# Moving two splits in VectorE's order in a transformer block with mixture of experts

## The chip, the cores and the metric

The kernel runs on one NeuronCore of a Trainium2 chip. The metric is the device time of one execution in microseconds; lower is better. All data is float32.

## The reference

Sixteen sequences of 512 tokens with 256 features pass one transformer block: attention with 16 heads of 64, then a feed-forward part with one shared expert and two of eight routed experts per token. Both parts stand behind a layernorm and are added to their input. Cut to what matters:

```python
def block(x):                                   # x: [16, 512, 256]
    n = layernorm(x)
    q, k, v = heads(n @ Wq.T), heads(n @ Wk.T), heads(n @ Wv.T)
    sim = 50 * tanh(q @ k.T * 64 ** -0.5 / 50)
    attn = softmax(where(causal, sim, -max))
    x = x + merge(attn @ v) @ Wo.T
    t = layernorm(x)
    shared = gelu(t @ sw1 + sb1) @ sw2 + sb2
    probs = softmax(t @ gate_w + gate_b)        # 8 experts, the best 2 are used
    routed = sum(probs[e] * (gelu(t @ w1[e] + b1[e]) @ w2[e] + b2[e]) for e in top2(probs))
    return x + routed + shared
```

## The kernel before

**Stages.** The kernel has two stages. In the first, some 2040 us, it goes through the sequences i = 0 to 15. Attention of a sequence is cut into eight pairs of heads, p = 0 to 7, and the feed-forward front of the sequence before (second layernorm, gate, choice of experts, shared expert) is woven between the pairs. In the second stage it runs the routed experts over gathered tiles of 128 tokens. The change touches the first stage only.

**High and low parts.** To keep float32 accuracy with a faster matmul type, every operand is split: the high part is a cast (`tensor_copy` to F32R), the low part is the original minus the high part. A product is made of high by high, high by low and low by high. Thus most results that leave TensorE's accumulators need a cast (ScalarE or VectorE) and a subtraction (VectorE) before TensorE can use them.

**The ring.** Scores, query and key projections, v, turned tokens, gate, hidden and shared output go through two accumulator slots in one fixed order (`ring_plan`, `AT`). TensorE may fill a slot when its content of two units ago has been emptied (`slot_for`), by ScalarE for scores, v and hidden, otherwise by VectorE. The shared output (`out`) of pair 7 takes the slot in which the queries and keys of the next sequence's pair 0 stood.

**Order.** Each engine runs its own fixed list; semaphores join them. VectorE's list for a pair p is in lines 980 to 1033:

- `weigh_values(i, c)` (L789) multiplies the attention output of chunk c by the inverse denominators; for even c it first takes the reciprocal (L796), the longest instruction of VectorE. A chunk holds half the features of four heads; there are eight per sequence. The chunk weighed in pair p >= 3 is p - 3. Chunks 5, 6 and 7 come in pairs 0 and 1 of the next sequence.
- `split_values(i, c)` (L803) casts the weighed chunk to `oT` high (L808) and subtracts for `oT` low (L810). There is one `oT`, so it waits on `projected` for TensorE's projection of the chunk before (`project_out`, L1268). TensorE projects chunk 6 in pair 2 and chunk 7 in pair 3 behind the scores.
- `empty_qk(i, p + 1)` (L776) makes the low parts of keys (L780) and queries (L785) for the next pair, once ScalarE has cast the high parts (L598, L602). The scores of that pair wait for it (`k_lo`, `dve_emptied`).
- in pair 1 the layernorm of sequence i + 1 (lines 1007 to 1012: statistics L727, Newton steps L748 to L754, application L760); its result is needed by `turn1(i + 1)` in pair 6.
- in pair 3 `add_attention(i - 1)` and the second layernorm; in pair 4 and 5 turned tokens and gate; in pair 6 `choose(i - 1)` (L857) and `split_hidden(i - 1)` (L839), which splits the shared expert's values after gelu for `shared_out` (L1303, high parts from L1305 on); in pair 7 the placing of tokens.

GpSimd masks probabilities and sums them over keys (L508, L520 to L526) for `denominators` (L1238), and sends rows to DRAM (L488, L497). ScalarE does tanh, exp, gelu and high parts. Queries and keys of pair p + 1 are projected in pair p.

Of the kernel before, what the change touches and what calls it, by code (L numbers as in the profile page):

```python
# [118 lines left out]
def block_program(nc, x, wqT, wkT, wvT, woT, gate_w, gate_b_rows, w1s, w1, w2s, w2,  # L119
# [4 lines left out]
    with ExitStack() as ctx:  # L124
# [593 lines left out]
        def _(dve):  # L718
            def split_lo(k):
                name, _ = parts[k]  # L720
                dve.wait_ge(hi_split, k + 1)
                nc.vector.tensor_tensor(split[name][1][:, :], raw[name][:, :],
                                        split[name][0][:, :].bitcast(F32), ALU.subtract).then_inc(lo_split, 1)

            def layernorm_stats(which, src):
                for t in range(NT):
                    last = nc.vector.bn_stats(ln[which]["stats"][:, t, :], src[:, t, :])  # L727
                last.then_inc(ln_steps[which], 1)

            def layernorm_guess(which, i):  # L730
                b, steps, done = ln[which], i * LN_STEPS, ln_steps[which]
                dve.wait_ge(done, steps + 1)
                for t in range(NT):
                    last = nc.vector.bn_aggr(b["mean_var"][:, t, :], b["stats"][:, t, :])
                last.then_inc(done, 1)
                dve.wait_ge(done, steps + 2)
                variance = b["mean_var"][:, :, 1:2]
                nc.vector.tensor_scalar(b["var_eps"][:, :, :], variance, EPS, None, ALU.add)
                nc.vector.tensor_scalar(b["minus_half"][:, :, :], variance, EPS, -0.5, ALU.add,
                                        ALU.mult).then_inc(done, 1)  # L740
                dve.wait_ge(done, steps + 3)
                nc.vector.tensor_scalar(b["rstd"][:, :, :].bitcast(I32), b["var_eps"][:, :, :].bitcast(I32), -0.5,
                                        RSQRT_GUESS, ALU.mult, ALU.add).then_inc(done, 1)
# [32 lines left out]
            def empty_qk(i, p):  # L776
                slot, done = ring[AT["qk", i, p, 0] % 2], 3 * (i * PAIRS + p)
                dve.wait_ge(qk_hi, done + 1)
                for h, r in enumerate(head_rows):
                    last = nc.vector.tensor_tensor(kT[head_rows[1 - h], h, :], slot[r, 1, :],  # L780
                                                   kT[r, h, :].bitcast(F32), ALU.subtract)
                last.then_inc(k_lo, 1)
                dve.wait_ge(qk_hi, done + 2)
                for h, r in enumerate(head_rows):
                    last = nc.vector.tensor_tensor(q_lo[r, h, :], slot[r, 0, :], qT[r, h, :].bitcast(F32),  # L785
                                                   ALU.subtract)
                last.then_inc(dve_emptied, 1)

            def weigh_values(i, c):  # L789

                g, quad = i * PAIRS + c, (i * PAIRS + c) // 2
                if c % 2 == 0:
                    if g >= 1:
                        dve.wait_ge(o_steps, 3 * g)
                    dve.wait_ge(den_done, quad + 1)
                    nc.vector.reciprocal(norm[:, :], bank_d[:, :]).then_inc(inverted, 1)  # L796
                    dve.wait_ge(inverted, quad + 1)
                dve.wait_ge(valued, g + 1)
                if g >= 1:
                    dve.wait_ge(o_steps, 3 * g)  # L800
                nc.vector.tensor_tensor(weighed[:, :], bank_o[:, :], norm[:, :], ALU.mult).then_inc(o_steps, 1)

            def split_values(i, c):  # L803
                g = i * PAIRS + c
                dve.wait_ge(o_steps, 3 * g + 1)
                if g >= 1:
                    dve.wait_ge(projected, g)
                nc.vector.tensor_copy(oT[0][:, :], weighed[:, :]).then_inc(o_steps, 1)  # L808
                dve.wait_ge(o_steps, 3 * g + 2)
                nc.vector.tensor_tensor(oT[1][:, :], weighed[:, :], oT[0][:, :].bitcast(F32),  # L810
                                        ALU.subtract).then_inc(o_steps, 1)
# [16 lines left out]
            def normalise_rows(i):  # L828
                if i >= 1:
                    dve.wait_ge(second_sent, i * NT * 16)  # L830
                layernorm_apply(2, i, row[:, :, TOKEN:TOKEN + D], stream, x2n_ready)
# [7 lines left out]
            def split_hidden(i):  # L839
                dve.wait_ge(act_emptied, EMPTIED[AT["hidden", i, 0, 0]][0])  # L840
                nc.vector.tensor_copy(hT[0][:, :, :], gelu[:, :, :]).then_inc(h_steps, 1)
                dve.wait_ge(h_steps, 2 * i + 1)
                nc.vector.tensor_tensor(hT[1][:, :, :], gelu[:, :, :], hT[0][:, :, :].bitcast(F32),
                                        ALU.subtract).then_inc(h_steps, 1)
# [3 lines left out]
            def empty_logits(i):  # L848
                n = AT["logits", i, 0, 0]
                gates = ring[n % 2][:, 0, 0:NT * E].rearrange("p (t e) -> p t e", t=NT)  # L850
                dve.wait_ge(ring_full, n + 1)
                nc.vector.tensor_reduce(norm1[:, :, :], gates, AX.X, ALU.max).then_inc(gate_steps, 1)
                dve.wait_ge(gate_steps, i * GATE_STEPS + 1)
                nc.vector.tensor_tensor(logit[:, :, :], gates, norm1[:, :, :].to_broadcast([P, NT, E]),
                                        ALU.subtract).then_inc(dve_emptied, 1)
# [124 lines left out]
            for i in range(NSEQ):  # L980
                for p in range(PAIRS):

                    chunk = (i, p - 3) if p >= 3 else (i - 1, p + 5)
                    if p == 2 or chunk[0] < 0:
                        chunk = None
                    if i >= 1 and p == 6:
                        empty_logits(i - 1)
                    if i == 0 and p == 3:
                        dve.wait_ge(idle_padded, 16 * 3)
                    if chunk is not None:  # L990
                        weigh_values(*chunk)
                        if chunk[1] % 2 == 0:
                            split_values(*chunk)
                    if p + 1 < PAIRS:
                        empty_qk(i, p + 1)
                    elif i + 1 < NSEQ:
                        empty_qk(i + 1, 0)
                    if chunk is not None and chunk[1] % 2 == 1:
                        split_values(*chunk)
                    if i == 0 and p <= 1:  # L1000
                        split_lo(3 + p)
                        if p == 1:
                            split_lo(5)
                    if p == 1 and i >= 1:
                        weigh_values(i - 1, PAIRS - 1)
                        split_values(i - 1, PAIRS - 1)
                    if p == 1 and i + 1 < NSEQ:
                        dve.wait_ge(xnext_loaded, 16 * (i + 2))
                        layernorm_stats(1, x_next)
                        layernorm_guess(1, i + 1)  # L1010
                        layernorm_newton(1, i + 1)
                        layernorm_apply(1, i + 1, x_next, x_next, xn_ready)
                    if p == 6 and i + 1 < NSEQ:
                        empty_turned1(i + 1)
                    if i == NSEQ - 1 and p in (4, 5, 6, 7):
                        prepare_bias(p - 4)
                    if i >= 1:
                        if p == 3:
                            add_attention(i - 1)
                            layernorm_guess(2, i - 1)  # L1020
                            layernorm_newton(2, i - 1)
                            normalise_rows(i - 1)
                        if p == 4:
                            empty_turned2(i - 1)
                        if p == 5:
                            empty_gate(i - 1)
                        if p == 6:
                            choose(i - 1)
                            split_hidden(i - 1)
                        if p == 7:  # L1030
                            empty_pos(i - 1)
                            add_shared(i - 1)
                            place_tokens(i - 1)
# [468 lines left out]
```

## Time and profile before

| | us |
|---|---|
| median of 3 runs | 2403.27 (2401.8 to 2406.9) |
| profiled execution | 2412.61 |
| its span, first to last instruction | 2410.9 |
| mean granted TensorE clock | 0.919 of 2.4 GHz |
| TensorE matmul busy | 1987.1 (82%) |
| VectorE busy | 1490.8 (62%) |
| ScalarE busy | 1425.9 (59%) |
| GpSimd busy | 1014.2 (42%) |

The rows come from one profiled execution. A timeline row gives start and duration in us, engine, line and operation, what is written and read, and how many instructions are merged (x); in square brackets stands the idle time of the engine just before, with what ended it. PE is TensorE's matmul, PEld its weight load, DVE VectorE, ACT ScalarE, POOL GpSimd. The granted clock is a share of 2.4 GHz; 0.50 is the level of 1.2 GHz.

### The profile page before, as it was taken

What the parts mean: (1) busy time and instruction counts of PE and PEld (TensorE: products, weight loads), DVE (VectorE), ACT (ScalarE), POOL (GpSimd) and SP (SyncE); (2) the same over time, 40 slices, a digit from 0 to 9 for tenths busy, and PEclk for the clock granted to TensorE, in tenths of its full rate; (3) what the DMA queues carried; (4) which work ended last, traced back from release to release, by engine and by line L of the source; (5) the groups of instructions that cost most, each with busy time, mean ns of one, the idle gap of its engine ahead of it and who ended that gap; (6) DMA issues with size and microseconds to landing.
All of it is one profiled execution on the core that took longest, in us unless ns stands there. A gap on an engine that the chain in (4) does not pass through costs nothing.

```text
span 2410.9 us, 39929 instructions
## 1 busy us (share of the span) xinstructions
PE 1987.1 (82%) x14653; PEld 1577.3 (65%) x14653; DVE 1490.8 (62%) x2803; ACT 1425.9 (59%) x2170; POOL 1014.2 (42%) x1195
## 2 busy tenths in 40 slices
PE   6788888887878788888888788898888885599898
PEld 5566666565656566666666666666665663499898
DVE  4657575756666666666665757575757577566565
ACT  6667475656566665666666657475766562244444
POOL 3434434343434434343434444444343443344344
PEclk9999899999999999999999999899999998699999
DMA  3000000000000000010100000000000002566464
GB/s 114 10 1 18 27 18 27 18 27 10 28 18 19 27 14 31 10 36 10 36 10 27 18 27 18 27 18 27 18 27 10 27 10 84 164 193 186 147 188 138
DMA packets 73665, 112.51 MB, mean 47 GB/s; under 512 B 9715, under 2 KB 52218, under 8 KB 73476
## 3 DMA queue, kind: packets, MB, share of 16 engines
q1 hardware_dynamic: 58468, 67.86, 9.8%
q0 software_dynamic: 15008, 42.10, 4.7%
q8 instruction: 123, 2.02, 0.4%
q14 instruction: 66, 0.54, 0.1%
HBM read 63.10 MB, written 48.65 MB: 46 GB/s over the span
## 4 chain that ended last, share of the span: by engine, by line
PE 52%; DVE 31%; ACT 11%; issue 4%; DMA 1%; another core or an unknown queue 0%; DVEq 0%; POOL 0%; SPq 0%; POOLq 0%; ACTq 0%
PE bank_o L1233 6%; PE ring L1212 6%; DVE q_lo L785 5%; PE ring L1191 5%; PE ring L1217 5%; DVE kT L780 4%; ACT prob L591 4%; PE ring L1139 3%; ACT prob L585 3%; PE ring L1140 3%; PE ring L1145 3%; PE ring L1198 2%; DVE norm L796 2%; ACT kT L598 2%; DVE stats L727 2%
## 5 line engine op out<-in xcount | busy, mean ns | idle before, releaser
L585 ACT ACTIVATE prob<-ring 128x1024 f32<-128x1024 f32 (+1 forms) x384 | 331.8, 880 | 538.2 <-PE ring L1217 533.2
L508 POOL TENSOR_SCALAR_AFFINE_SELECT prob<-prob 128x256 f32<-128x256 f32 x512 | 233.6, 472 | 884.8 <-ACT prob L591 883.9
L1212 PE MATMUL ring<-qT,kT 128*128 128x256 f32 (+3 forms) x1024 | 258.2, 357 | 185.0 <-DVE q_lo L785 133.9
L1212 PEld LDWEIGHTS ring<-qT,kT 128*128 128x128 f32 x1024 | 183.8, 206 | 270.9 <-DVE q_lo L785 133.8
L591 ACT ACTIVATE prob<-prob 128x1024 f32<-128x1024 f32 (+1 forms) x384 | 344.0, 913 | 5.3
L520 POOL TENSOR_TENSOR key_sum<-prob 128x768 f32<-128x768 f32 x128 | 235.2, 1838 | 223.2 <-PE bank_d L1247 211.4
L1233 PE MATMUL bank_o<-prob,v 128*32 128x512 f32 (+3 forms) x4096 | 304.8, 438 | 20.8 <-DVE oTh L808 8.3
L780 DVE TENSOR_TENSOR kT<-ring,kT 64x512 fp32r<-64x512 f32 x256 | 176.4, 689 | 227.4 <-ACT kT L598 224.2
L808 DVE CAST oTh<-weighed 128x512 fp32r<-128x512 f32 x128 | 65.3, 510 | 284.1 <-PE acc L1264 280.8
L1217 PE MATMUL ring<-q_lo,kT 128*128 128x256 f32 (+3 forms) x1024 | 239.1, 336 | 0.0
L1233 PEld LDWEIGHTS bank_o<-prob,v 128*32 128x32 f32 x4096 | 117.1, 110 | 181.0 <-issue 157.6
L796 DVE RECIPROCAL norm<-bank_d 128x512 f32<-128x512 f32 x64 | 214.6, 3353 | 6.2 <-remote 5.2
L1217 PEld LDWEIGHTS ring<-q_lo,kT 128*128 128x128 f32 x1024 | 183.3, 203 | 13.2
L785 DVE TENSOR_TENSOR q_lo<-ring,qT 64x512 fp32r<-64x512 f32 x256 | 176.3, 689 | 8.3 <-ACT qT L602 2.6
L523 POOL TENSOR_TENSOR key_sum<-key_sum,prob 128x512 f32<-128x512 f32 x128 | 169.5, 1324 | 10.0
L598 ACT CAST kT<-ring 64x512 fp32r<-64x512 f32 x256 | 148.1, 579 | 32.5 <-PE ring L1145 31.0
L602 ACT CAST qT<-ring 64x512 fp32r<-64x512 f32 x256 | 148.8, 581 | 24.9 <-PE ring L1145 21.6
L608 ACT CAST qT<-qT 64x512 fp32r<-64x512 f32 x256 | 158.1, 618 | 5.4
L1256 PE MATMUL ring<-w_2h,x2Tl 128*128 128x256 f32 x128 | 55.2, 432 | 121.3 <-DVE q_lo L785 119.2
L1256 PE MATMUL acc<-w_oh,oTh 128*128 128x256 f32 x512 | 132.3, 293 | 0.6 <-DVE oTh L808 0.6
L1258 PE MATMUL acc<-w_ol,oTh 128*128 128x256 f32 x512 | 125.7, 280 | 0.0
L1256 PEld LDWEIGHTS ring<-w_2h,x2Tl 128*128 128x128 f32 x128 | 41.1, 321 | 123.0 <-DVE q_lo L785 120.8
(224 smaller groups left out, 4835.5 us busy)
## 6 DMA issues: line engine op xcount, KB each, us to landing
xin<-first SPq DMA_DIRECT2D x71, 257.0 KB
xin<-second SPq DMA_DIRECT2D x71, 129.0 KB
xin<-base SPq DMA_DIRECT2D x71, 128.0 KB
x_next<-in_x SPq DMA_DIRECT2D x16, 512.0 KB, 4.6
x_res<-in_x SPq DMA_DIRECT2D x16, 512.0 KB, 5.1
raw_e<-in_w SPq DMA_DIRECT2D x4, 1024.0 KB, 6.6
first<-pad SPq DMA_DIRECT2D x9, 257.0 KB, 8.7
second<-pad SPq DMA_DIRECT2D x9, 129.0 KB, 7.7
```

Source lines behind the costliest of these rows:

```text
L508: last = nc.gpsimd.affine_select(out=diag, in_=diag, compare_op=ALU.is_ge, fill=0.0, base=0, pattern=[[0, 2], [1, P]], channel_multiplier=-1)
L520: nc.gpsimd.tensor_tensor(sums[:, :, :], t0[:, :, P:N], t13[:, :, 0:N - P], ALU.add).then_inc(sum_steps, 1)
L585: nc.scalar.activation(probs[p % PROBS][u][:, :, :], slot[:, :, 0:UNIT_COLS[u]], ACT.Tanh, scale=SCALE / SOFTCLAMP).then_inc(act_emptied, 1)
L591: nc.scalar.activation(cols, cols, ACT.Exp, scale=SOFTCLAMP).then_inc(exp_done, 1)
L598: last = nc.scalar.copy(kT[r, h, :], slot[r, 1, :])
L780: last = nc.vector.tensor_tensor(kT[head_rows[1 - h], h, :], slot[r, 1, :], kT[r, h, :].bitcast(F32), ALU.subtract)
L785: last = nc.vector.tensor_tensor(q_lo[r, h, :], slot[r, 0, :], qT[r, h, :].bitcast(F32), ALU.subtract)
L796: nc.vector.reciprocal(norm[:, :], bank_d[:, :]).then_inc(inverted, 1)
L1212: pe.matmul(slot[:, h, to], kT[:, h, keys], qT[:, h, q], start=k == 0, stop=False)
L1217: last = pe.matmul(slot[:, h, to], kT[:, h, keys], q_lo[:, h, q], start=False, stop=k == len(tiles) - 1)
L1233: last = pe.matmul(bank_o[h * QD:(h + 1) * QD, j * P:N], v[:, j, f:f + QD], probs[(2 * quad + h // 2) % PROBS][u][:, h % 2, at:at + N - j ...
L1256: pe.matmul(dst[:, t // 2, t % 2, :], a[0][:, here], w[0], start=start and t % 2 == 0 and k == 0, stop=False)
```

## The change

Two calls in VectorE's list move; no instruction and no wait is added or removed. `split_values(i - 1, 7)` moves from pair 1, where it stood between the weighing of chunk 7 and the layernorm of sequence i + 1, to pair 2, behind `empty_qk(i, 3)`. `split_hidden(i - 1)` moves from behind `choose(i - 1)` in pair 6 to ahead of `empty_qk(i, 7)` in the same pair.

```diff
@@ -991,6 +991,8 @@
                         weigh_values(*chunk)
                         if chunk[1] % 2 == 0:
                             split_values(*chunk)
+                    if p == 6 and i >= 1:
+                        split_hidden(i - 1)
                     if p + 1 < PAIRS:
                         empty_qk(i, p + 1)
                     elif i + 1 < NSEQ:
@@ -1003,6 +1005,7 @@
                             split_lo(5)
                     if p == 1 and i >= 1:
                         weigh_values(i - 1, PAIRS - 1)
+                    if p == 2 and i >= 1:
                         split_values(i - 1, PAIRS - 1)
                     if p == 1 and i + 1 < NSEQ:
                         dve.wait_ge(xnext_loaded, 16 * (i + 2))
@@ -1026,7 +1029,6 @@
                             empty_gate(i - 1)
                         if p == 6:
                             choose(i - 1)
-                            split_hidden(i - 1)
                         if p == 7:
                             empty_pos(i - 1)
                             add_shared(i - 1)
```

## Rows read from the trace of the kernel before

**Rows 1.** Page, part 1: busy time, share of the span, instructions of each engine.

```profile
PE 1987.1 (82%) x14653; PEld 1577.3 (65%) x14653; DVE 1490.8 (62%) x2803; ACT 1425.9 (59%) x2170; POOL 1014.2 (42%) x1195
```

**Rows 2.** TensorE's waits: who for whom, total us, times, longest us.

```profile
PE ring L1212 <- DVE q_lo L785: 133.9, 17, 8.8
PE ring L1256 <- DVE q_lo L785: 119.2, 14, 8.6
```

**Rows 3.** Stretches: start:end, length, engines' busy us, clock, DMA share, GB/s.

```profile
809.68:936.01 126.33, 104.00 (x756) 79.05 (x757) 79.32 (x146) 78.89 (x108) 53.13 (x64) 0.92 0.06 22
...
1820.04:1937.93 117.89, 104.06 (x756) 79.08 (x757) 71.18 (x122) 78.96 (x108) 49.84 (x62) 0.94 0.05 19
```

**Rows 4.** Timeline of VectorE, sequence 6, pair 1 to pair 3.

```profile
780.17 0.69 DVE L801 TENSOR_TENSOR weighed<-bank_o,norm 128x512 f32<-128x512 f32 x1 [1.87 <-remote]
797.23 0.43 DVE L808 CAST oTh<-weighed 128x512 fp32r<-128x512 f32 x1 [16.36 <-PE acc L1264]
...
798.30 1.40 DVE L727 BATCH_NORM_STATS2 stats<-x_next 128x6 f32<-128x256 f32 x4
...
801.02 1.80 DVE L754 SCALAR_TENSOR_TENSOR rstd<-newton,rstd 128x4 f32<-128x4 f32 x1
...
806.82 1.39 DVE L780 TENSOR_TENSOR kT<-ring,kT 64x512 fp32r<-64x512 f32 x2
```

**Rows 5.** Timeline of the other engines in that stretch.

```profile
788.90 0.98 POOL L497 DMA_INDIRECT first<-row,slot_ids  x1 [0.30 <-issue]
...
791.80 1.16 ACT L598 CAST kT<-ring 64x512 fp32r<-64x512 f32 x2
...
800.04 0.86 PE L1247 MATMUL bank_d<-key_sum,ones 128*32 128x384 f32 x8
```

**Rows 6.** Timeline of TensorE, first scores of pairs 3 and 4, sequences 6 and 15.

```profile
809.68 0.79 PE L1212 MATMUL ring<-qT,kT 128*128 128x256 f32 x2 [8.79 <-DVE q_lo L785]
...
821.05 0.47 PE L1212 MATMUL ring<-qT,kT 128*128 128x256 f32 x2 [0.34 <-ACT qT L608]
...
1937.93 0.51 PE L1212 MATMUL ring<-qT,kT 128*128 128x256 f32 x2 [0.38 <-DVE q_lo L785]
...
1947.59 0.48 PE L1212 MATMUL ring<-qT,kT 128*128 128x256 f32 x2 [0.34 <-ACT qT L608]
```

**Rows 7.** Stretches around both stalls; the granted clock is third from the end.

```profile
809.70:813.50 3.80, 3.80 (x13) 3.41 (x14) 3.77 (x2) 2.08 (x3) 0.41 (x1) 0.50 0.00 0
...
871.20:872.20 1.00, 0.00 (x0) 0.00 (x0) 0.97 (x2) 0.00 (x0) 0.92 (x2) 0.73 0.00 0
...
876.70:881.50 4.80, 4.77 (x22) 4.77 (x23) 0.36 (x2) 0.00 (x0) 0.00 (x0) 0.50 0.00 0
```

**Rows 8.** Timeline of VectorE, sequence 6, pairs 6 and 7.

```profile
856.23 1.39 DVE L780 TENSOR_TENSOR kT<-ring,kT 64x512 fp32r<-64x512 f32 x2 [5.90 <-ACT kT L598]
...
866.43 0.69 DVE L841 CAST x2Tl<-gelu 128x1024 fp32r<-128x1024 f32 x1
...
868.38 3.35 DVE L796 RECIPROCAL norm<-bank_d 128x512 f32<-128x512 f32 x1
...
872.49 0.62 DVE L808 CAST oTh<-weighed 128x512 fp32r<-128x512 f32 x1
```

**Rows 9.** Timeline of ScalarE and TensorE in those pairs.

```profile
846.68 1.27 ACT L618 ACTIVATE gelu<-ring,b1s 128x512 f32<-128x512 f32 x2 [2.02 <-PE ring L1145]
...
876.73 0.58 PE L1256 MATMUL ring<-w_2h,x2Tl 128*128 128x256 f32 x1 [8.58 <-DVE q_lo L785]
```

**Rows 10.** Timeline of VectorE: splits beside GpSimd's work, sequences 7 and 15.

```profile
899.86 0.95 DVE L808 CAST oTh<-weighed 128x512 fp32r<-128x512 f32 x1
...
1995.88 2.38 DVE L810 TENSOR_TENSOR oTl<-weighed,oTh 128x512 fp32r<-128x512 f32 x1
```

**Rows 11.** Timeline of TensorE, end of sequence 15.

```profile
2025.91 3.75 PE L1233 MATMUL bank_o<-prob,v 128*32 128x512 f32 x32 [5.84 <-DVE weighed L801]
```

**Rows 12.** Page, part 6: DMA issues, KB each, median us to landing.

```profile
first<-pad SPq DMA_DIRECT2D x9, 257.0 KB, 8.7
```

## Prediction

> **What bounds the kernel now.** I read the page's busy line first, then TensorE's waits, then the span of one sequence, then the timeline around each long wait. TensorE is busy 82% of the span and VectorE 62% [rows 1], so TensorE carries the time and the question is what keeps it idle. The list of its waits has two entries far ahead of the rest, both on the second low-part instruction of VectorE (L785): 133.9 us ahead of score matmuls, 119.2 us ahead of the shared output product [rows 2]. Each is one stall per sequence of about 8.8 and 8.6 us. A sequence lasts 126.3 us from its pair-3 scores to the next sequence's; the last such stretch lasts 117.9 us [rows 3]. That is 8.4 us less, and its one difference up to that point is that sequence 15 normalises no successor in pair 1. The kernel itself thus shows what the first stall is worth.
>
> First stall (sequence 6 as the pattern). VectorE weighs chunk 7 at 780.17 us, then its split stands idle 16.36 us, because the split may overwrite oT only when TensorE has projected chunk 6, at 797.2. Queued behind that split are the layernorm of the next sequence (from 798.30) and the low parts of pair 3 (from 806.82 until TensorE starts) [rows 4]. TensorE finished the denominators at 800.9 [rows 5] and stands 8.79 us until 809.68 [rows 6]. So a wait that concerns nobody in a hurry (chunk 7 is projected only after the scores of pair 3) holds 8.5 us of layernorm and 2.8 us of urgent low parts.
>
> Second stall. In pair 6 and 7 VectorE runs without a gap from 856.23 to 876.7: low parts of pair 7, split of chunk 3, turned tokens, choice of experts, split of the shared values (866.43 to 868.38), reciprocal, weighing and split of chunk 4, low parts of the next sequence's pair 0 [rows 8]. TensorE waits 8.58 us for the last of these, because the shared product needs the ring slot that they empty [rows 9].
>
> **The change part by part.** Nothing is added or removed: 2803 VectorE instructions before and after, no DMA and no wait is new, and the only queue whose order changes is VectorE's own.
>
> Move 1, chunk 7's split (L808, L810, 1.1 us) goes behind the low parts of pair 3. The layernorm then starts at 780.9 and takes the 8.5 us it takes now, up to 789.4. Some of its tiny instructions are stretched now, the longest to 1.80 us [rows 4], while GpSimd sums keys; at the new place it sums the keys of another pair, so I keep the duration. Next come the low parts, which need ScalarE's high part of the keys: that copy starts at 791.80 and takes 1.16 us [rows 5]. So they run from 793.0 to 795.8 and are done 5.0 us before TensorE is free at 800.8. The split waits for 797.2 as before and ends at 798.4, ahead of the reciprocal (801.0) and of its projection (after three score units, about 803.4). The new wait stands in front of the reciprocal only, which needs the denominators of 800.9 anyway. The layernorm has 3.5 us of idle and 5.0 us of slack behind it: it could last 17.1 us, twice its length, before TensorE notices. If that cover were gone, the move would cost one for one. GpSimd issues its last row write to `first` by 789.9 [rows 5]; the residual addition needs it landed, now at 821.1 and then at about 810.5. That leaves 20 us, and writes to `first` of twice that size land in 8.7 us [rows 12].
>
> The stall itself is 8.79 us. Besides, TensorE comes out of it at a granted clock of 0.50, the 1.2 GHz level, for some 3.9 us [rows 7]. From the scores of pair 3 to those of pair 4 it takes 11.37 us in sequence 6; in sequence 15, with no stall ahead, 9.66 us [rows 6]. That is 1.71 us more, and sequence 15 also shows what is late next: pair 4's scores wait 0.34 us for ScalarE, nothing longer. Sum of move 1: 14 sequences (1 to 14) x (8.79 + 1.71) = 147.0 us, and 0.4 us for sequence 15, where the split alone held the low parts.
>
> Move 2, the shared values' split (1.95 us from its start to the reciprocal) goes ahead of pair 7's low parts. After weighing chunk 3 VectorE idles 5.90 us, from 850.33 until 856.23 [rows 8]. The gelu it reads ended at 847.95 [rows 9], so it fits at 850.3 to 852.3 and is hidden by that gap; without the gap it would cost the same 1.95 us that it saves. The chain behind it starts 1.95 us earlier: the denominators, chunk 4's products and ScalarE's copies were all ready several microseconds before VectorE came to them, so none of them ends last instead.
>
> What eats into it: chunk 4's split then meets GpSimd's key sums. Its cast took 0.62 us [rows 8], beside such sums 0.95 us in pair 0 of the next sequence, and a subtraction behind it up to 2.38 us instead of 0.69 [rows 10]. So the loss is between 0 and 1.7 us per sequence. I take 0.5, near the cast's own excess over its undisturbed 0.43 us. The Trainium skill (SBUF — State Buffer, section Who interferes with whom) has VectorE and GpSimd share one port pair as an exclusive lock that a cast takes, so that the second to issue waits for the whole of the other instruction. By that rule the cast would wait for the end of the sum in flight and the subtraction behind it for the next; if it did so for two whole sums, move 2 would bring nothing, which is the second rival below.
>
> Sum of move 2: 14 x (1.95 - 0.5) = 20.3 us. In sequence 15 no low parts hold the product, but the chain leads on to chunk 5's weighing, for which TensorE waits 5.84 us at 2025.91 [rows 11]: 1.9 us.
>
> **Total:** 147.0 + 0.4 + 20.3 + 1.9 = 169.6 us. The profiled execution took 2412.6 us (span 2410.9), so it would take 2243.0. It stands 9.3 us above the median of the runs; the saving is idle time, so I subtract it from the median: 2403.3 - 169.6 = 2233.7 us.
>
> What stays unknown is the clock after the second stall. It shrinks from 8.6 to about 7.1 us; TensorE now runs on at 0.50 for some 5.1 us behind it, and for 3.9 us behind the first [rows 7]. Every sequence gets shorter by a tenth, so where the clock falls and rises against the work will shift. A difference of 1.2 us at half speed is 0.6 us, 14 x 0.6 = 8 us either way. With 0 to 1.7 for the loss the case spans 147.4 + 1.9 + 14 x (0.25 to 1.95) -/+ 8, so savings of 145 to 185 us: 2218 to 2258.
>
> **The rivals.**
> First rival: the clock no longer falls in the shortened second stall. It fell some 3.5 us into the present one (0.73 on average from 871.2 to 872.2 [rows 7]), so 7 us should still do; but were it to stay up, half of 5.1 us comes back as well, 14 x 2.55 = 36 us: 2198 us. Likewise, if the first stall's place left a short wait, nothing would change here. Chance 0.07.
>
> Second rival: move 2 brings nothing, because contention with the key sums takes the whole 1.95 us or another releaser (ScalarE's copies, denominators) holds the low parts. Then 147.4 + 1.9 = 149.3: 2254 us. For it: GpSimd is busy through that stretch and 2.38 us was seen once [rows 10]. Against it: usual excesses are 0.2 to 0.5 us. Chance 0.12.
>
> Third rival: move 1 doesn't do what it says; the stall is held by something that the waits do not name (the v copy, a ring slot), and only move 2 counts: 2403.3 - 22.2 = 2381 us. Against it stands sequence 15, where exactly this stall is 0.38 us. Chance 0.03.
>
> Fourth rival, slower: the layernorm at its new place runs beside GpSimd's key sums and its four indirect row writes, and they stretch it. Up to 17.1 us nothing shows; from there each further microsecond comes out of TensorE, and at 17.1 + 12.0 = 29.1 us the gain of both moves is gone. At 32 us it would be 14 x 2.9 = 41 us slower: 2444 us. Now its longest stretch is 1.80 us for one tiny instruction [rows 4], so this needs a dozen of them. Chance 0.01.
>
> **How the numbers follow.** The forecast has 0.77, the rivals 0.07, 0.12, 0.03 and 0.01. Likeliest: 2233.7 us. Range: 2210 to 2258; it holds the forecast and the second rival and leaves out the other three. A difference of 0.2%, about 5 us, is what a measurement of this kernel can tell from none. Every case but the fourth is faster by more: faster 0.98, same 0.01 (the fourth short of its end), slower 0.01.
>
> **What would show it.** In the profile after: the wait of score matmuls on L785 (133.9 us) falls below 20 us, and the split's idle time of 16 us before it shrinks to about 1.3 us; the layernorm (L727 on x_next) follows the weighing of chunk 7 directly; a sequence lasts 126.3 - 10.5 - 1.5 = 114.3 us; the wait of the shared product falls from 8.6 to about 7.1 us each; the clock is 1.00 over pair 3. Wrong would be: a new wait of over 1 us ahead of pair 3's or pair 7's scores, a layernorm of over 17 us, or a second stall that stays at 8.6.

## The result, and the profile after

The changed kernel takes 2226.96 us (median of 4 runs, 2224.22 to 2230.45), the kernel before 2403.4 us (2401.8 to 2406.9). The ratio is 0.9265, with a 95% interval of 0.9247 to 0.9283. The saving at the medians is 176.4 us, where 169.6 us were forecast; 2227.0 lies inside the range of 2210 to 2258. The profiled execution took 2224.22 us, with a span of 2222.5 us and a mean granted clock of 0.955 (0.919 before).

Page of the changed kernel, part 1 (to compare with [rows 1]):

```profile
PE 1945.4 (88%) x14653; PEld 1539.9 (69%) x14653; DVE 1501.1 (68%) x2803; ACT 1421.8 (64%) x2170; POOL 1004.9 (45%) x1195
```

The counts are the same, as announced. TensorE is busy 88% of the span instead of 82%, and 41.7 us shorter in total: that part isn't idle time but matmuls that ran at a higher clock. VectorE grew by 10 us. Nearly all of it stands in the splits of the weighed chunks, whose subtractions (L810) take 101.6 instead of 93.7 us and whose casts (L808) take 66.9 instead of 65.3; what they meet at their new time is shown at the end of this section.

TensorE's waits of the changed kernel (who for whom, total us, times, longest us), to compare with [rows 2]. The edit moved TensorE's lines down by two: scores are L1214 now, the shared product L1258.

```profile
PE ring L1258 <- DVE q_lo L785: 98.9, 14, 7.1
PE ring L1214 <- DVE x2Tl L773: 20.4, 15, 7.8
...
PE ring L1214 <- DVE q_lo L785: 10.5, 2, 7.9
```

The scores' wait of 133.9 us is down to 10.5 us, in two waits that both belong to the start of the kernel (22 and 71 us into it). The shared product's wait went from 119.2 to 98.9 us, or from 8.5 to 7.07 us each. The 20.4 us for L773 were there before as well (20.6 us). What is new are single waits of under 3 us in the last sequence.

VectorE's timeline of the changed kernel, sequence 6, pair 1 to pair 3 (start, us, instruction, idle time before it), to compare with [rows 4]:

```profile
712.05 0.69 DVE L801 TENSOR_TENSOR weighed<-bank_o,norm 128x512 f32<-128x512 f32 x1
712.65 1.40 DVE L727 BATCH_NORM_STATS2 stats<-x_next 128x6 f32<-128x256 f32 x4
...
714.58 1.84 DVE L739 TENSOR_SCALAR minus_half<-mean_var 128x4 f32<-128x4 f32 x1
...
719.84 1.38 DVE L760 TENSOR_SCALAR x_next<-x_next,mean_var,rstd 128x256 f32<-128x256 f32 x4
726.70 1.39 DVE L780 TENSOR_TENSOR kT<-ring,kT 64x512 fp32r<-64x512 f32 x2 [5.48 <-ACT kT L598]
728.12 1.39 DVE L785 TENSOR_TENSOR q_lo<-ring,qT 64x512 fp32r<-64x512 f32 x2
730.93 0.43 DVE L808 CAST oTh<-weighed 128x512 fp32r<-128x512 f32 x1 [1.42 <-PE acc L1266]
731.39 0.69 DVE L810 TENSOR_TENSOR oTl<-weighed,oTh 128x512 fp32r<-128x512 f32 x1
734.73 3.36 DVE L796 RECIPROCAL norm<-bank_d 128x512 f32<-128x512 f32 x1 [2.64 <-PE bank_d L1249]
```

The layernorm (L727 to L760) follows the weighing of chunk 7 with no gap and takes 8.6 us. The low parts of pair 3 are done at 729.5, 5.0 us before TensorE is free. The split idles 1.42 us where it idled 16.36 us, and its end at 732.1 leaves 2.6 us to the reciprocal. TensorE's timeline of the same sequence, first scores of pair 3 and of pair 4, and the stretch that they bound (start:end, length, busy us of PE, PEld, DVE, ACT, POOL, granted clock, DMA share, GB/s):

```profile
734.53 0.50 PE L1214 MATMUL ring<-qT,kT 128*128 128x256 f32 x2
...
744.19 0.47 PE L1214 MATMUL ring<-qT,kT 128*128 128x256 f32 x2 [0.34 <-ACT qT L608]
```

```profile
733.50:744.19 10.69, 10.35 (x96) 7.19 (x85) 8.19 (x8) 8.43 (x12) 8.25 (x9) 1.00 0.00 0
```

Pair 3 starts with no wait at a clock of 1.00, and pair 4 follows after 9.66 us: to the hundredth what sequence 15 of the kernel before showed [rows 6], and 1.71 us less than its sequence 6.

VectorE's timeline of the changed kernel, the same sequence, pairs 6 and 7 [rows 8], and the shared product that it releases [rows 9]:

```profile
773.37 0.69 DVE L841 CAST x2Tl<-gelu 128x1024 fp32r<-128x1024 f32 x1
...
779.36 1.39 DVE L780 TENSOR_TENSOR kT<-ring,kT 64x512 fp32r<-64x512 f32 x2 [4.04 <-ACT kT L598]
...
789.56 3.35 DVE L796 RECIPROCAL norm<-bank_d 128x512 f32<-128x512 f32 x1
...
793.67 0.64 DVE L808 CAST oTh<-weighed 128x512 fp32r<-128x512 f32 x1
794.35 1.09 DVE L810 TENSOR_TENSOR oTl<-weighed,oTh 128x512 fp32r<-128x512 f32 x1
```

```profile
798.34 0.58 PE L1258 MATMUL ring<-w_2h,x2Tl 128*128 128x256 f32 x1 [7.05 <-DVE q_lo L785]
```

The split of the shared values sits in the gap, which shrank from 5.90 to 4.04 us. In the chain behind it the subtraction of chunk 4 took 1.09 us instead of 0.69. GpSimd's timeline beside it shows why:

```profile
792.76 1.26 POOL L523 TENSOR_TENSOR key_sum<-key_sum,prob 128x512 f32<-128x512 f32 x1
794.11 0.79 POOL L526 TENSOR_TENSOR key_sum<-key_sum,prob 128x256 f32<-128x256 f32 x1
```

The cast, issued at 793.67, finds a sum in flight that ends at 794.02, and itself ends 0.29 us later, at 794.31. The subtraction finds the next sum, which ends at 794.90, and itself ends at 795.44. Undisturbed the two take 0.43 and 0.69 us, so each ends 0.14 or 0.15 us earlier than if its work had begun only when the sum in flight was over.

### The profile page after: what moved, and what is told of

It is laid out like the page before. It is cut to its first block, busy times and chain, and to the rows that moved or that the text cites. A ratio compares the mean times of both kernels' runs of the same rounds, so it can differ in the third digit from the quotient of the medians.

```text
span 2222.5 us, 39929 instructions
## 1 busy us (share of the span) xinstructions
PE 1945.4 (88%) x14653; PEld 1539.9 (69%) x14653; DVE 1501.1 (68%) x2803; ACT 1421.8 (64%) x2170; POOL 1004.9 (45%) x1195
## 3 DMA queue, kind: packets, MB, share of 16 engines
q1 hardware_dynamic: 58468, 67.86, 10.6%
## 4 chain that ended last, share of the span: by engine, by line
PE 56%; DVE 27%; ACT 13%; issue 3%; DMA 1%; POOL 0%; DVEq 0%; SPq 0%; POOLq 0%
PE bank_o L1235 8%; PE ring L1193 5%; ACT prob L591 5%; DVE q_lo L785 5%; PE ring L1214 5%; ACT prob L585 4%; DVE kT L780 4%; PE ring L1219 4%; PE ring L1141 3%; PE ring L1142 3%; PE ring L1147 3%; PE ring L1200 3%; DVE norm L796 2%; ACT kT L598 2%; DVE oTl L810 2%
## 5 line engine op out<-in xcount | busy, mean ns | idle before, releaser
L508 POOL TENSOR_SCALAR_AFFINE_SELECT prob<-prob 128x256 f32<-128x256 f32 x512 | 224.0, 454 | 713.4 <-ACT prob L591 713.2
L1214 PE MATMUL ring<-qT,kT 128*128 128x256 f32 (+3 forms) x1024 | 241.3, 338 | 61.2 <-DVE x2Tl L773 20.4
L1214 PEld LDWEIGHTS ring<-qT,kT 128*128 128x128 f32 x1024 | 168.0, 190 | 146.4 <-issue 74.7
L1219 PE MATMUL ring<-q_lo,kT 128*128 128x256 f32 (+3 forms) x1024 | 227.7, 324 | 0.0
L1219 PEld LDWEIGHTS ring<-q_lo,kT 128*128 128x128 f32 x1024 | 173.0, 191 | 11.5
L785 DVE TENSOR_TENSOR q_lo<-ring,qT 64x512 fp32r<-64x512 f32 x256 | 176.3, 689 | 6.5 <-ACT qT L602 0.8
L1258 PE MATMUL ring<-w_2h,x2Tl 128*128 128x256 f32 x128 | 53.9, 424 | 99.7 <-DVE q_lo L785 98.9
L1258 PE MATMUL acc<-w_oh,oTh 128*128 128x256 f32 x512 | 132.0, 292 | 0.6 <-DVE oTh L808 0.6
L581 ACT COPY v<-ring 128x1024 f32<-128x1024 f32 x64 | 64.9, 1014 | 82.7 <-PE ring L1200 82.3
L1258 PEld LDWEIGHTS ring<-w_2h,x2Tl 128*128 128x128 f32 x128 | 40.4, 316 | 101.3 <-DVE q_lo L785 100.5
```

The lines of the kernel that those rows point to most:

```text
L508: last = nc.gpsimd.affine_select(out=diag, in_=diag, compare_op=ALU.is_ge, fill=0.0, base=0, pattern=[[0, 2], [1, P]], channel_multiplier=-1)
L1214: pe.matmul(slot[:, h, to], kT[:, h, keys], qT[:, h, q], start=k == 0, stop=False)
L1219: last = pe.matmul(slot[:, h, to], kT[:, h, keys], q_lo[:, h, q], start=False, stop=k == len(tiles) - 1)
L1258: pe.matmul(dst[:, t // 2, t % 2, :], a[0][:, here], w[0], start=start and t % 2 == 0 and k == 0, stop=False)
```

## The experiments

Edits are shown against the changed kernel, except where said otherwise. Ratios are to the kernel before, run on the same chip beside each.

### Each move by itself

Move 1 alone has the shared values' split back behind the choice:

```diff
-                    if p == 6 and i >= 1:
-                        split_hidden(i - 1)
...
                         if p == 6:
                             choose(i - 1)
+                            split_hidden(i - 1)
```

> Move 1 alone (chunk 7's split behind the low parts of pair 3); the shared values' split stays behind the choice of experts. My theory, two independent stalls: the first stall of 8.79 us and its slow matmuls (1.71 us) go, the second stays at 8.5 us: 147 us off, 2403 to about 2256, ratio 0.939. Rival, a shared cause (one move only pays with the other): less than 100 us off.

Measured: 2263.39 us, ratio 0.9402 (0.9389 to 0.9415), 144.4 us under the 2407.84 us beside it.

Move 2 alone has chunk 7's split back in pair 1:

```diff
                     if p == 1 and i >= 1:
                         weigh_values(i - 1, PAIRS - 1)
-                    if p == 2 and i >= 1:
                         split_values(i - 1, PAIRS - 1)
```

> Move 2 alone (the shared values' split ahead of pair 7's low parts); chunk 7's split stays in pair 1. My theory: the second stall falls from 8.5 to about 7.1 us and the first stays at 8.8: 14 x 1.45 + 1.9 = 22 us off, ratio 0.991, and with the clock's shifts between 0.987 and 0.995. Rival, the moved split only moves the load to another place of the same chain: no change, ratio 1.000.

Measured: 2380.3 us, ratio 0.9883 (0.9867 to 0.9898), 27.5 us less; 22 were expected, and 0.987 to 0.995 with the clock's shifts. TensorE's waits, first of move 1 alone, then of move 2 alone:

```profile
PE ring L1257 <- DVE q_lo L785: 119.4, 14, 8.6
```

```profile
PE ring L1213 <- DVE q_lo L785: 133.9, 17, 8.8
PE ring L1257 <- DVE q_lo L785: 99.0, 14, 7.1
```

Each move takes away its own stall and leaves the other's as it was. The two savings add up to 172.0 us; both together gave 176.4. So they hardly depend on each other. The second and the third rival fall here: move 2 brings 27.5 us by itself, and move 1 removes just the stall that it was aimed at.

### How much layernorm fits at the new place

The forecast counts 8.6 us of cover (3.5 us idle and 5.0 us of slack). Unused reciprocals of 3.36 us each use it up, n = 2 or 4 of them in each pair 1 of i = 1 to 14, ahead of the layernorm of sequence i + 1:

```diff
+                        if i + 1 < NSEQ:
+                            dve.wait_ge(o_steps, 3 * (i * PAIRS - 1) + 1)
+                            for k in range(n):
+                                nc.vector.reciprocal(norm[:, :], raw_like).then_inc(filled_up, 1)
+                                dve.wait_ge(filled_up, n * (i - 1) + k + 1)
```

> The changed kernel with two reciprocals of 3.35 us each put ahead of the layernorm of sequences 1 to 14, on VectorE (6.7 us, their results are not used). My theory: the layernorm has 8.6 us of slack (3.5 us idle before the low parts and 5.0 us between them and TensorE), so nothing waits: the same time as the changed kernel within 0.3%, ratio to before about 0.927. Rival, the layernorm's length sits on the path in some sequences, or GpSimd is disturbed: each us costs 14, so 40 to 90 us more.

Measured: 2233.41 us, ratio 0.9274 (0.9261 to 0.9286), whose interval holds the changed kernel's 0.9265. VectorE's timeline, pair 1 to 3:

```profile
719.02 6.74 DVE L1013 RECIPROCAL norm<-w_kh 128x512 f32<-128x512 f32 x2
725.79 1.41 DVE L728 BATCH_NORM_STATS2 stats<-x_next 128x6 f32<-128x256 f32 x4
...
731.84 1.39 DVE L781 TENSOR_TENSOR kT<-ring,kT 64x512 fp32r<-64x512 f32 x2
```

The 5.48 us idle before the low parts have gone, and nothing has reached TensorE: 14 x 6.74 = 94 us of work cost nothing that can be told apart.

> As the one before with four reciprocals (13.4 us). My theory: 13.4 - 8.6 = 4.8 us stick out in each of 14 sequences, so TensorE waits about 4.8 us ahead of the scores of pair 3, 67 us more than the changed kernel, and 0 to 24 us on top if the clock falls in that wait: 2294 to 2318 us. Rival, no slack: 14 x 13.4 = 188 us more, 2415 us.

Measured: 2293.46 us, ratio 0.9527 (0.9512 to 0.9542). TensorE's timeline at pairs 3 and 4:

```profile
761.33 0.51 PE L1221 MATMUL ring<-qT,kT 128*128 128x256 f32 x2 [2.18 <-DVE q_lo L786]
...
772.19 0.47 PE L1221 MATMUL ring<-qT,kT 128*128 128x256 f32 x2 [1.55 <-DVE kT L781]
773.57 0.51 PE L1226 MATMUL ring<-q_lo,kT 128*128 128x256 f32 x2 [0.90 <-DVE q_lo L786]
```

The sum is 4.63 us in this sequence. On average over the trace a sequence lasts 118.27 us instead of 113.75, which is 63 us in 14, and the ratios of the runs differ by as much (0.9527 - 0.9265 = 0.0262, or 63 us). The total is as worked out (a load of 13.5 + 8.5 us on 17.1 us of cover), but its form is not, so part of the agreement is luck. Only 2.18 us stand where I had put all of it. The layernorm itself is down to 5.8 us there (752.58 to 758.42), because no key sums run beside it; the split, which had been hidden between the low parts and the reciprocal, now pushes the reciprocal and with it the low parts of pair 4, which shows as 1.55 and 0.90 us. It and the split of the next chunk take 2.5 and 2.6 us there instead of 1.1, because they now run beside key sums.

The clock fell too. Of the twelve waits of 2.18 us seven left it at 1.00, as in the sequence shown, where it fell only at 773.99, at the waits of pair 4. At the other five it fell as TensorE came out of the wait, as here:

```profile
644.39 0.80 PE L1221 MATMUL ring<-qT,kT 128*128 128x256 f32 x2 [2.18 <-DVE q_lo L786]
```

```profile
644.40:647.40 3.00, 3.00 (x9) 2.61 (x10) 2.93 (x3) 1.27 (x3) 2.26 (x3) 0.50 0.00 0
```

In those five pair 4 has no wait for the low parts of over 0.5 us: TensorE is late there by its own slow clock.

### Is it the clock that gave the rest?

TensorE gets 52 unused matmuls behind the counting of earlier tokens, so that it works through most of the second stall:

```diff
-                pe.matmul(slot[:, 1, 0:K * NT * E], ones_r[:, :], flags, start=True, stop=True).then_inc(ring_full, 1)
+                last = pe.matmul(slot[:, 1, 0:K * NT * E], ones_r[:, :], flags, start=True, stop=True)
+                for k in range(52 if i + 1 < NSEQ else 0):
+                    last = pe.matmul(slot[:, k % 2, 256:N], ones_r[:, :], w_2[0][:, 0, :], start=True, stop=True)
+                last.then_inc(ring_full, 1)
```

> The changed kernel with 52 more matmuls of 256 columns (results not used) between the counting of earlier tokens and the shared product of sequences 0 to 13, so that TensorE is busy while it waits for the ring slot; they end before the slot is free. My theory: the slow shared product (4.8 to 6.1 us, 5.36 on average) is the 1.2 GHz clock after an idle stretch; with the idle stretch filled it takes about 3.3 us at a granted clock of 1.00, 14 x 2.1 = 29 us off the changed kernel's 2227: 2198, although it does more work. Rival, the product is slow for its operands or weight loads: no gain, 2227 or slower.

Measured: 2204.53 us, ratio 0.9172 (0.9159 to 0.9184): 22 us faster than the changed kernel, with more work. TensorE's timeline, then the product's stretch (start:end, length, PE busy, granted clock, DMA share, GB/s):

```profile
669.90 6.16 PE L1323 MATMUL ring<-w_2h,ones_r 128*128 128x256 f32 x52
677.23 0.38 PE L1258 MATMUL ring<-w_2h,x2Tl 128*128 128x256 f32 x1 [1.17 <-DVE q_lo L785]
```

```profile
677.23:680.77 3.54, 3.54 (x29) 1.00 0.00 0
```

The product ran at 1.00 and took 3.54 us. The same 28 matmuls in the changed kernel, in three sequences that follow each other, took this (all engines' columns):

```profile
683.85:689.91 6.06, 6.06 (x28) 5.92 (x28) 0.33 (x2) 0.00 (x0) 0.00 (x0) 0.53 0.00 0
798.34:803.57 5.23, 5.23 (x28) 5.10 (x28) 0.33 (x2) 0.00 (x0) 0.00 (x0) 0.63 0.00 0
912.00:916.79 4.79, 4.79 (x28) 4.66 (x28) 0.34 (x2) 0.00 (x0) 0.00 (x0) 0.70 0.00 0
```

Their mean is 5.36 us. So the clock costs 1.82 us per sequence or 25 us in 14, of which the runs return 22; 29 were expected, from a product of 3.3 us. The filling has a price as well. The edit also reaches a fifteenth product, that of sequence 14, ahead of which TensorE waits for the choice of experts and not for the slot:

```profile
1805.43 7.80 PE L1323 MATMUL ring<-w_2h,ones_r 128*128 128x256 f32 x52
```

There the unused matmuls fill nothing: the product starts 5.0 us later (127.0 us after the one before, instead of 122.0) and runs 1.5 us faster, so some 3.5 us are given away.

The first rival (the clock stays up) did not come true in the changed kernel, where the clock still fell at every stall of 7.07 us. Its price of 36 us was too high besides: it had 5.1 us at half speed, worth 2.55 us a sequence, where 1.82 were lost: the 28 matmuls would take 7.1 us if all ran at half speed, and took 4.8 to 6.1.

### The other place for the shared values' split

Here the split stands between pair 7's low parts and the choice, so it is neither in the idle gap nor behind the choice:

```diff
                         if p == 6:
+                            split_hidden(i - 1)
                             choose(i - 1)
```

(and no longer ahead of `empty_qk(i, 7)`).

> The changed kernel, but the shared values' split stands directly ahead of the choice of experts and behind pair 7's low parts, chunk 3's split and the turned tokens. My theory: what move 2 gains is the idle gap ahead of pair 7's low parts and not the order against the choice; here the split is back in the unbroken chain, so the second stall is 8.5 us again and the time that of move 1 alone, ratio 0.940. Rival, the gain comes from freeing the stretch between the choice and the reciprocal: ratio 0.927 as for the changed kernel.

Measured: 2272.29 us, ratio 0.9446 (0.9433 to 0.9459). TensorE's timeline:

```profile
228.32 0.27 PE L1319 MATMUL ring<-chosen,earlier 128*128 128x64 f32 x1 [2.29 <-DVE chosen L883]
...
236.25 0.58 PE L1257 MATMUL ring<-w_2h,x2Tl 128*128 128x256 f32 x1 [7.55 <-DVE q_lo L785]
```

The stall is 9.8 us in two pieces. The choice now comes late as well, and VectorE's timeline says why it is worse than a mere exchange: beside GpSimd's sums the split took 3.6 us instead of 1.95 (and the last flags 1.85 instead of 0.27):

```profile
219.44 1.38 DVE L841 CAST x2Tl<-gelu 128x1024 fp32r<-128x1024 f32 x1
220.86 2.19 DVE L843 TENSOR_TENSOR x2Th<-gelu,x2Tl 128x1024 fp32r<-128x1024 f32 x1
```

It is slower than move 1 alone, by 11 us after the ratios (0.9446 against 0.9402; the medians, from different chips, differ by 9). The longer split is in all 14 sequences: 1.36 or 1.38 us for the cast, 2.19 for the subtraction. Move 2's gain hangs on the idle gap that it fills, not on the order of split and choice.

### What holds the second stall

What is left of it is 7.07 us behind the low parts of the next sequence, and ahead of these stand the reciprocal, weighing and split of chunk 4, 5.9 us from 789.56 to 795.44 in the changed kernel's timeline of sequence 6. In the next experiment the low parts go first:

```diff
+                    if p == PAIRS - 1 and i + 1 < NSEQ:
+                        empty_qk(i + 1, 0)
                     if chunk is not None:
                         weigh_values(*chunk)
...
-                    elif i + 1 < NSEQ:
-                        empty_qk(i + 1, 0)
```

> The changed kernel, and in pair 7 VectorE makes the low parts of the next sequence's pair 0 ahead of weighing and splitting chunk 4 (reciprocal 3.35, weighing 0.69, split 1.7 us). My theory: the second stall is the rest of this chain; it falls from 7.1 to about 2.6 us (ScalarE's high parts then come last), the clock does not fall in so short a stall, so the shared product takes 3.3 instead of 5.4 us, and chunk 5's values wait about 0.6 us for the weighing instead: 14 x 5.9 = 83 us off, about 2144 us, ratio 0.892. Rival, the reciprocal only changes places and TensorE waits as long for chunk 4's weighing: 2227 us.

Measured: 2166.79 us, ratio 0.9017 (0.9004 to 0.9029), 60 us under the changed kernel, but 23 us above what I expected. TensorE's timeline at the shared product and in sequence 0, then two stretches of the product:

```profile
672.29 0.39 PE L1258 MATMUL ring<-w_2h,x2Tl 128*128 128x256 f32 x1 [2.60 <-DVE q_lo L785]
```

```profile
131.01 3.72 PE L1235 MATMUL bank_o<-prob,v 128*32 128x512 f32 x32 [6.85 <-DVE weighed L801]
```

```profile
672.30:674.00 1.70, 1.70 (x11) 1.70 (x12) 1.70 (x1) 0.00 (x0) 0.91 (x2) 0.74 0.00 0
674.00:676.00 2.00, 2.00 (x11) 2.00 (x11) 1.97 (x2) 0.00 (x0) 0.00 (x0) 0.50 0.00 0
```

The stall is 2.60 us, as expected. What I had wrong is the clock. I took for granted that so short a wait would leave it up, but it falls some 0.8 us into the product, which takes 5.04 us. So it goes in 13 of the 14 sequences; in one, at 1108.30 us, it stayed up and the product took its 3.6 us. Besides, sequence 0 has no shared product that needs the low parts early, and there the new order only makes the values wait 6.85 us, and they then take 3.72 us instead of 2.36. Sequences 1 to 14 are 4.85 us shorter on average, 68 us in all; less the 8 us of sequence 0 that is the 60 measured.

The next two leave sequence 0 as it was, and the second of them fills the wait of 2.6 us with 18 unused matmuls, built as the 52 above:

```diff
+                    if p == PAIRS - 1 and 1 <= i < NSEQ - 1:
+                        empty_qk(i + 1, 0)
...
-                    elif i + 1 < NSEQ:
+                    elif i == 0:
                         empty_qk(i + 1, 0)
```

> As the kernel with low parts ahead of chunk 4's weighing in pair 7, but sequence 0 keeps the old order, since it has no shared product to cover the weighing and waited 6.85 us for it. My theory: 5 to 7 us less than there, 2161 us, ratio 0.899. Rival, the first sequence's wait was covered: no difference, 0.902.

> The same with 18 unused matmuls of 256 columns (2.1 us) in the 2.6 us in which TensorE waits ahead of the shared product. I had expected no fall of the clock there, yet the product took 5.0 us of 2.6 us of idle time before it. My theory: the idle time alone brings the fall, so with it filled the product takes 3.5 us: 14 x 1.5 = 21 us less than without, 2140 us, ratio 0.890. Rival, the fall has another cause (a fixed rhythm, the load of the product itself): no gain.

Measured: 2155.93 us, ratio 0.8966 (0.8953 to 0.8978), and 2148.81 us, ratio 0.8937 (0.8925 to 0.8949). By the medians the old order in sequence 0 is worth 10.9 us (12 by the ratios, for the two ran on different chips), where 5 to 7 were expected. In the traces the first shared product starts 8.6 us earlier, of which 8.2 are the wait of 6.85 us and the slow values behind it (1.36); the rest of the medians' difference is not located. Timeline of TensorE and stretches of the filled version:

```profile
546.20 2.29 PE L1325 MATMUL ring<-w_2h,ones_r 128*128 128x256 f32 x18
548.95 0.38 PE L1260 MATMUL ring<-w_2h,x2Tl 128*128 128x256 f32 x1 [0.46 <-DVE q_lo L785]
...
553.06 2.36 PE L1237 MATMUL bank_o<-prob,v 128*32 128x512 f32 x32 [0.51 <-DVE weighed L801]
```

```profile
549.00:552.40 3.40, 3.40 (x28) 3.35 (x28) 3.37 (x2) 0.00 (x0) 0.86 (x2) 1.00 0.00 0
548.95:657.05 108.10, 102.19 (x774) 77.23 (x774) 79.21 (x146) 78.75 (x108) 52.70 (x65) 1.00 0.08 25
```

The product is back at 1.00 in all 14 sequences, which rules out a fixed rhythm and the load of the product itself, and it ends 1.4 us earlier. Of that 7.1 us in all reach the end by the medians (0.80 us per sequence between the two traces, 11 us in 14), where 21 us were expected: the values that follow now wait 0.51 us for chunk 4's weighing, which is next in line. Here too the unused matmuls reach the fifteenth product, where nothing needs them and they cost about 1 us. This version is the fastest here, 10.6% under the kernel before and 3.6% under the changed one.

The changed kernel ran once more beside these three:

> The changed kernel itself beside the two below: the reference for them on one chip, ratio 0.9265 as measured before.

Measured: 2229.01 us, ratio 0.927 (0.9258 to 0.9283). The result repeats.

## Why the prediction was right, and where not

**Move 1.** The stall of 8.79 us and the 1.71 us of slow clock behind it both went, as the prediction's row of sequence 15 had promised; 9.66 us from pair 3 to pair 4 in either. Move 1 alone gave 144.4 us at the medians against 147.4 in the sum. In its profile the second stall stayed at 8.5 us, but the product behind it took longer, about 6.1 instead of 5.8 us (the mean from the first matmul of the product to the first of the values, 14 sequences each): some 4 us given back by where the clock happens to fall.

**Move 2.** TensorE's wait for the product went from 119.2 / 14 = 8.51 us to 98.9 / 14 = 7.06, so 1.45 us less; 1.95 - 0.5 = 1.45 was forecast. The 0.5 for contention is borne out by 0.64 and 1.09 us against 0.62 and 0.69 [rows 8]: 0.42. That it fits so closely is in part luck, for it was put near one cast's excess and not worked out from when the sums run. The second rival feared that each of the two instructions waits for a whole sum. What each waits for is the rest of the sum in flight: in the first 2000 us of the kernel before, 155 of VectorE's 156 instructions that are stretched by over 0.1 us start while one of GpSimd's is in flight, and 110 of these end 0.13 to 0.16 us earlier than that one's end plus their own undisturbed time. The trace thus agrees with the rule of the Trainium skill (SBUF — State Buffer, section Who interferes with whom), by which the second to issue is blocked until the other's instruction is done; the prediction's two whole sums were an upper bound of it. At the other place of the shared values' split, where the sums in flight are longer, the same rule gives the 1.38 and 2.19 us.

**The cover.** I had 3.5 us idle and 5.0 us of slack with a layernorm of 8.5 us; it is 5.48, 5.0 and 8.6. The idle part is longer since the weighing of chunk 7 no longer waits 1.87 us ahead of itself [rows 4]. That wait is back in the traces of each move alone and of both fillings, in 13 sequences each; what it is for no run shows. The fourth rival is out: the longest of the tiny instructions takes 1.85 us, and the two fillings show that 6.74 us more are free and that some 17 us between weighing and pair 3 is the limit.

**Clock behind the second stall.** This was the term of +/- 8 us, and it came out in favour of the change. In the kernel before the product and what follows up to the values takes 5.82 us on average over 14 sequences, in the changed kernel 5.38: 14 x 0.44 = 6.1 us, close to the 6.8 us by which the medians' saving exceeds the forecast. These stretches repeat in threes, the length of a sequence with them:

```profile
683.85:798.34 114.49, 102.49 (x757) 77.70 (x757) 79.94 (x146) 78.68 (x108) 52.41 (x64) 0.96 0.07 24
798.34:912.00 113.66, 101.65 (x756) 76.87 (x756) 80.11 (x146) 78.67 (x108) 52.32 (x64) 0.97 0.07 24
912.00:1025.19 113.19, 101.12 (x757) 76.37 (x757) 79.94 (x146) 78.62 (x108) 52.39 (x64) 0.97 0.07 24
```

Their mean is 113.8 us; 114.3 was forecast from 126.3 [rows 3].

**Rest.** In sequence 15, from the shared product at 1887.03 to the values of chunk 5 at 2025.91 [rows 11], the kernel before takes 138.88 us and the changed one 135.65 (1707.90 to 1843.55). That is 3.2 us less, where 2.3 were forecast; the wait of 5.84 us is 4.81 now, and TensorE reaches it earlier. From there to the last product the two take 39.7 and 36.5 us, but that stretch can't be compared: with the same code in it, it lasts 36.5 us in the repeated run of the changed kernel, 38.5 with four reciprocals and 42.2 with two.

The traces differ by 188.4 us and the medians by 176.4. Of these 12 us 3.9 lie ahead of the first move: the stall at the start began at 74.43 us before and at 70.52 after. The other traces, with the same code up to there, have it between 70.2 and 74.8, so this is a difference between executions and not the change. Another 3 us lie in the experts' stage; the remaining 5 are not located. So the agreement per sequence is good to about 0.5 us (12.5 us measured, 12.0 forecast), and single traces can't settle more. The range's lower end of 2210 us stood 8 us below the 2218 that the terms give, with no term for it; it was not needed.

## What to carry to other kernels

An instruction that waits for a buffer which is free late, on work that is needed late, should stand behind everything that is needed soon on its engine: the price of the wrong place was not the split's 1.1 us but 8.8 us of idle TensorE and 1.7 us of slow clock, per sequence. Look for a stretch of the same trace in which the suspected wait is missing (here the last sequence), and take from it what the change is worth and what ends last then. Before a stall is left as "only 2.6 us", read the granted clock behind it, and try unused matmuls in it, only where TensorE would wait: they gave 22 us at one length of stall and 7 us at another, and cost 3.5 us at the one place where there was nothing to fill.

## What the runs showed of the hardware

- The granted clock can fall to the 1.2 GHz level behind 2.60 us of idle TensorE (0.50 from 674.00 on, above), and did so in 13 of 14 sequences. Behind waits of 2.18 us in the kernel with four reciprocals it fell in five of twelve and stayed at 1.00 in seven. So neither is a safe length, and the same wait can go either way. The Trainium skill (TensorE: Matmul & The Clock Gate, section A second HAM failure mode: psum-queue depth-cycling) tells of another kernel in which frequent small idle times between groups of matmuls make the clock swing between its two levels; the trace agrees in the swing, while here one wait per sequence was enough.
- The same stall of 7.07 us costs 4.79, 5.23 or 6.06 us of product, by turns. A kernel of equal sequences isn't equal to the clock.
- Some of VectorE's instructions stretch beside GpSimd's, even the tiniest: 0.16 to 1.85 us for 4 elements per partition, 0.27 to 1.85 us for the two of the flags, 1.22 to 2.19 us for the subtraction of 1024. They are casts, operations with a scalar, and those that read two operands from SBUF. Those that read one of their operands from an accumulator keep their time beside the same sums: all 256 of L785 take 0.68 to 0.70 us, 66 of them with one of GpSimd's in flight.
